# A layer of scan attention and a mixture of experts in one kernel: six wide shared slots first, six lone expert blocks in a row, weights asked for ahead of rows, and another engine for the last sums

## The chip, the cores and the metric

The kernel runs on one core of a Trainium2 chip. The metric is the time of one execution on the device in microseconds (us); the median of three runs is compared. A core has TensorE (PE, matrix products; PEld is its weight load), VectorE (DVE), ScalarE (ACT), GpSimd (POOL) and SyncE (SP), each with its own instruction stream that runs in order; they meet at semaphores. Here SP issues almost all DMAs (SPq in the rows), and POOL issues the gathers and scatters.

## The reference

```
x = x + attn(layernorm(x))      # x: 4 x 1024 x 256, 4096 rows in all
x = x + ffn(layernorm(x))

attn: h = rmsnorm(.)*gamma;  q, kv, a = split(h @ w_qkva.T);  a = sigmoid(a)
      y[t] = a[t]*y[t-1] + kv[t];  return q*y
ffn:  logits = rows @ router_w.T             # 7 routed experts, the best 2 per row
      w = softmax(the two logits)
      mixed = sum over both of w * (silu(g)*u) @ w_down[e]   # g, u = rows @ w_gate[e], w_up[e]; hidden 1024
      mixed += the same form with the shared expert, for all rows
```

## The kernel before, in words

Each float32 product is made from three products of rounded parts (high x high, high x low, low x high), so every weight needs a rounded copy (ACT, `round_w`, L809) and a remainder (`w_lo`: POOL's `split_lo`, L627, for gate and down, DVE's `split_up`, L1694, for up). Raw weights come into `w_raw`, which lies where the remainder will be.

After the attention part (to about 105 us) the expert work is one sequence of *slots* of 256 rows, numbered n. TensorE runs a slot alone (`slot`), or two of them as a *quad* of 512 rows (`quad`): eight steps j, each with 12 gate and up products (L1145, or L1101 in a slot), then the down product for the first and the second pair of row tiles. For the down product there is a wide form (`down_wide`, L1123 and L1126: one product of 512 columns, one of 256) and a narrow one (L1167: three of 256). TensorE may begin step j only when DVE has *gated* step j-2 (silu times up, L1733, after ACT's silu, L865 or L837). Then ACT rounds the gated values (L872, L844) and DVE takes the remainder (L1739).

The order of the slots, all written out by hand:

* n = 0, 1: shared expert, slots. n = 2, 4, 6, 8: shared expert, quads. Between their steps DVE works out the routing (functions in `betweens`: places, one-hot `hot_rows` and `hot_cols` for eight lists, `take_lists`, `take_targets`, `owners`), and TensorE turns each one-hot pair into a list (`list_part`, L1076).
* n = 10, 11: the first two *lone* blocks: 128 rows of one expert with weights of its own, in plain float32 (`lone`, L1187 and L1195), weights in `w_spare` (`load_lone`, L449 and L452 on SP). That memory holds the routing's tables before.
* n = 12 (`LATE`): a shared quad. n = 14 to 17: four more lone blocks.
* from `R0` = 18: 12 routed quads, then 8 routed slots (`PAIRED`), a new expert's weights for each of these 20 *turns*.
* `NB0`: two last shared quads. While they run, each row's two expert results come back from DRAM (`got`, `load_got`, L539 and L542 on SP), are weighed and added. Of 32 row tiles, DVE mixes 12 (`mix`, L1679, two instructions a tile); ACT weighs the other 20 (`weigh`, L924) and POOL adds them (L714, L716) into `resid`, which SP stores.

SP's order in the loop over the eight routed slots is: `load_down` for the next turn, `put_and_load` (store gathered rows once POOL's gather has landed, then load them turned, L457 and L463), and only then `load_gate_up` for the turn after the next (L414), which needs the end of this slot's gate and up products. Before the first lone block SP does: put and load of the first two lone blocks' rows, put of two more, wait for `routed`, `load_lone(0)` (L449), the rows of n = 12, 13, `load_lone(1)`.

POOL's order in one of those turns is `split_lo` of gate, gather, `split_lo` of down, scatter. The last stores wait until the sums for their rows are made.

Of the kernel before, what the change touches and what calls it, by code (L numbers as in the profile page):

```python
# [11 lines left out]
ALU = mybir.AluOpType  # L12
# [10 lines left out]
def preln_scan_moe_kernel(nc, x, w_qkva, gamma, router_w, w_gate, w_up, w_down,  # L23
# [9 lines left out]
    JH = H // P  # L33
# [21 lines left out]
    assert len(LONES) == NS and R0 % 2 == 0 and NS % 2 == 0 and TURNS % 2 == 0  # L55
# [7 lines left out]
    assert OTHERS[0] <= 4 and OTHERS[3] == 0  # L63
# [26 lines left out]
    with ExitStack() as ctx:  # L90
# [213 lines left out]
        others_summed = sem("others_summed")  # L304
        others_mixed = sem("others_mixed")
# [52 lines left out]
        def _(sp):  # L358
# [116 lines left out]
            for n in range(2, FIRST_LONE):  # L475
                load_x(n, n, z_dram, n % 2)
# [35 lines left out]
            for j in range(PAIRED):  # L512
                r, n, u = QUADS + j, R0 + 2 * QUADS + j, j % 2
                load_down(r + 1, 1 - u, n, shared_rows if r + 1 == TURNS else None)
                v = n + 4 - R0
# [4 lines left out]
                if r + 2 <= TURNS:  # L520
                    load_gate_up(r + 2, u, n + 1, shared_rows if r + 2 == TURNS else None)
# [27 lines left out]
            sp.wait_ge(mixed, TOP * (ST + OTHERS[0]))  # L549
# [3 lines left out]
            sp.wait_ge(mixed, TOP * (ST + OTHERS[0] + ST))  # L553
            load_got(3)
            store_own(1)
            for j in (1, 2):
                sp.wait_ge(others_mixed, FROM[j + 1] - FROM[1])
                store_others(j)
# [5 lines left out]
        def _(pool):  # L564
# [140 lines left out]

            for j in (1, 2):
                for b in range(2):
                    many = OTHERS[j] // 2
                    ps_ = slice(ST + b * many, ST + (b + 1) * many)
                    t = FROM[j] + b * many  # L710
                    done = FROM[j] - FROM[1] + (b + 1) * many
                    rows, sums = resid[:, t:t + many, :], got[:, j % 2, ps_, 0, :]
                    pool.wait_ge(weighed, TOP * done)
                    pool.tensor_tensor(sums, sums, got[:, j % 2, ps_, 1, :], ALU.add).then_inc(others_summed, many)  # L714
                    pool.wait_ge(others_summed, done)
                    pool.tensor_tensor(rows, rows, sums, ALU.add).then_inc(others_mixed, many)  # L716

        @block.scalar
        def _(act):
# [176 lines left out]
            for n in range(2, FIRST_LONE - 2, 2):  # L896
                quad(n, n % 4, early=True)
            quad(FIRST_LONE - 2, (FIRST_LONE - 2) % 4, turns=(), early=True)
            for i in range(2):
                lone(i)  # L900
            quad(LATE, LATE % 4, turns=())
# [16 lines left out]
            def weigh(j, ps_):  # L918
# [8 lines left out]
            quad(NB0, NB0 % 4, between={6: lambda: weigh(1, (ST,)), 7: lambda: weigh(1, (ST + 1,))})  # L927
            weigh(1, range(ST + 2, ST + OTHERS[1]))
            quad(NB0 + 2, (NB0 + 2) % 4, turns=(), between={
                j: lambda j=j: weigh(2, (ST + j,)) for j in range(JH)})  # L930
            weigh(2, range(ST + JH, ST + OTHERS[2]))

        @block.tensor
        def _(pe):
# [195 lines left out]
            def quad(n, h, buf, m=None, between=(), skip=NS, ahead=2, early=False):  # L1130
# [29 lines left out]
                for t in range(ST, 2 * ST):  # L1160
                    for j in range(JH):
                        if not early:
# [42 lines left out]
            for n in range(2, FIRST_LONE, 2):  # L1205
# [3 lines left out]
            for i in range(2):  # L1209
                lone(i)  # L1210
# [719 lines left out]
```

## Time and the profile before

| | us |
|---|---|
| median of three runs | 1050.58 (1049.94 to 1053.31) |
| the profiled execution, whole | 1051.96 |
| its span, first to last instruction | 1050.2 |
| PE / PEld / DVE busy | 990.5 / 859.6 / 594.0 |
| ACT / POOL busy | 474.5 / 419.2 |
| mean granted TensorE clock | 0.975 |

Busy time of TensorE is that of pipelined instructions, whose modelled ends overlap; a stage's length and the idle time before a group tell more. The granted clock is a share of 2.4 GHz, 0.5 being 1.2 GHz.

### The profile page before, as it was taken

The page shows a single profiled execution, that of the slowest core. Times are in us where ns is not written, and L with a number is a line of the kernel's source. Part 1 is how long each engine was busy: PE and PEld are TensorE (multiplying, and loading weights), DVE is VectorE, ACT ScalarE, POOL GpSimd, SP SyncE. Part 2 cuts the span into 40 slices and gives each one's busy share as a digit, 9 for nine tenths or more (in the row PEclk, how much of TensorE's full clock was granted, in tenths as well). Part 3 has the DMA queues.
Part 4 walks back from the last instruction along what each step waited for, and adds up shares of the span by engine and source line. Part 5 has one row for each costly group of instructions (what it writes and reads, how often), then busy time and mean ns, then how long its engine had stood idle before and what let it go on. Part 6 is the DMA issues. An engine that isn't in the chain of part 4 may idle for free.

```text
span 1050.2 us, 15774 instructions
## 1 busy us (share of the span) xinstructions
PE 990.5 (94%) x5517; PEld 859.6 (82%) x5517; DVE 594.0 (57%) x1048; ACT 474.5 (45%) x754; POOL 419.2 (40%) x267
## 2 busy tenths in 40 slices
PE   7999999999969999999999999999999798999966
PEld 6788988788868998888888888888889688898755
DVE  7987677778514244445644456444564343555744
ACT  4555343422213325544655446544464444765532
POOL 2335000000201233546556464654646565674304
PEclk9999999999989999999999999999999898999979
DMA  9333200000297675464345543455444556673362
GB/s 311 101 81 81 81 21 21 21 1 2 56 315 259 222 243 170 160 195 153 117 169 170 190 153 112 168 172 190 133 129 158 173 175 214 223 257 98 113 229 71
DMA packets 145905, 155.05 MB, mean 148 GB/s; under 512 B 75321, under 2 KB 134210, under 8 KB 138690
## 3 DMA queue, kind: packets, MB, share of 16 engines
q1 hardware_dynamic: 139120, 136.08, 39.8%
q0 software_dynamic: 6720, 18.36, 5.5%
q8 instruction: 27, 0.44, 0.2%
q14 instruction: 20, 0.16, 0.1%
q10 hardware_dynamic: 18, 0.01, 0.0%
HBM read 127.67 MB, written 26.74 MB: 147 GB/s over the span
## 4 chain that ended last, share of the span: by engine, by line
PE 67%; DVE 11%; issue 8%; POOL 5%; DMA 4%; ACT 2%; SPq 1%; DVEq 0%; POOLq 0%; ACTq 0%
PE ps L1145 32%; PE ps L1123 11%; PE ps L1126 6%; PE ps L1101 5%; PE ps L1187 4%; PE ps L1007 3%; POOL w_both L627 3%; PE ps L1195 2%; DMA got<-expert_rows 2%; DVE y_sb L1333 2%; PE ps L991 1%; DVE resid L1679 1%; PE ps L1167 1%; DVE h_early L1733 1%; DVE h_lo L1739 1%
## 5 line engine op out<-in xcount | busy, mean ns | idle before, releaser
L1145 PE MATMUL ps<-xs_hi,w_both 128*128 128x512 f32 x1216 | 384.7, 394 | 12.5 <-DVE ps L1733 11.8
L1145 PEld LDWEIGHTS ps<-xs_hi,w_both 128*128 128x128 f32 x1216 | 230.6, 190 | 63.2 <-DVE ps L1733 13.1
L627 POOL TENSOR_TENSOR w_both<-w_raw,w_both 128x2048 fp32r<-128x2048 f32 x45 | 224.2, 4981 | 129.7 <-ACT w_both L809 121.2
L1123 PE MATMUL ps<-w_both,h_hi 128*128 128x512 f32 x704 | 250.2, 399 | 1.0 <-DVE h_lo L1739 0.9
L1145 PE MATMUL ps<-xs_lo,w_both 128*128 128x512 f32 x608 | 238.6, 392 | 0.0
L1126 PE MATMUL ps<-w_both,h_lo 128*128 128x256 f32 x704 | 197.5, 281 | 0.0
L1739 DVE TENSOR_TENSOR h_lo<-ps,h_hi 128x512 fp32r<-128x512 f32 x152 | 105.1, 692 | 126.9 <-ACT h_hi L872 80.3
L651 POOL DMA_INDIRECT x_stage<-z_rows,idx_x x70 | 73.1, 1044 | 240.4 <-DVE idx_x L1651 156.4
L1733 DVE TENSOR_TENSOR ps<-ps,silu 128x512 f32<-128x512 f32 x152 | 106.2, 699 | 109.2 <-ACT silu L865 79.1
L1123 PEld LDWEIGHTS ps<-w_both,h_hi 128*128 128x128 f32 x704 | 132.5, 188 | 33.6 <-DVE h_lo L1739 1.8
L865 ACT ACTIVATE silu<-ps 128x512 f32<-128x512 f32 x152 | 90.7, 597 | 135.4 <-PE ps L1145 135.3
L1101 PE MATMUL ps<-xs_hi,w_both 128*128 128x256 f32 x640 | 126.3, 296 | 17.7 <-DVE ps L1733 16.8
L809 ACT ACTIVATE w_both<-w_raw 128x1024 fp32r<-128x1024 f32 x126 | 130.5, 1053 | 25.1 <-DMA w_raw<-in_L_ffn_w_gate_dram 25.0
L1145 PEld LDWEIGHTS ps<-xs_lo,w_both 128*128 128x128 f32 x608 | 115.5, 190 | 23.4
L1126 PEld LDWEIGHTS ps<-w_both,h_lo 128*128 128x128 f32 x704 | 133.0, 189 | 0.7
L1101 PEld LDWEIGHTS ps<-xs_hi,w_both 128*128 128x128 f32 x640 | 106.6, 202 | 19.8 <-DVE ps L1733 17.6
L664 POOL DMA_INDIRECT expert_rows<-y_rows,idx_y x70 | 69.6, 995 | 132.6 <-DMA expert_rows<-y_rows,idx_y 81.6
L872 ACT ACTIVATE h_hi<-ps 128x512 fp32r<-128x512 f32 x120 | 71.8, 598 | 71.4 <-DVE ps L1733 71.3
L1101 PE MATMUL ps<-xs_lo,w_both 128*128 128x256 f32 x320 | 93.9, 293 | 0.0
L1101 PEld LDWEIGHTS ps<-xs_lo,w_both 128*128 128x128 f32 x320 | 64.7, 202 | 0.0
L1809 DVE TENSOR_TENSOR y_rows<-ps,y_rows 128x512 f32<-128x512 f32 x24 | 16.6, 692 | 75.2 <-ACT y_rows L888 59.5
L1187 PE MATMUL ps<-xs_lone,w_spare 128*128 128x128 f32 x384 | 45.5, 281 | 9.1 <-issue 9.1
(225 smaller groups left out, 1055.4 us busy)
## 6 DMA issues: line engine op xcount, KB each, us to landing
w_raw<-in_L_ffn_w_gate_dram SPq DMA_DIRECT2D x20, 1024.0 KB, 5.0
w_raw<-in_L_ffn_w_up_dram SPq DMA_DIRECT2D x20, 1024.0 KB, 7.3
w_raw<-in_L_ffn_w_down_dram SPq DMA_DIRECT2D x20, 1024.0 KB, 7.0
sorted_rows<-x_stage SPq DMA_DIRECT2D x32, 256.0 KB, 2.2
x_rows<-sorted_rows SPq DMA_DIRECT2D x128, 64.0 KB, 2.0
w_spare<-in_L_ffn_w_up_dram SPq DMA_DIRECT2D x6, 1024.0 KB, 5.2
w_spare<-in_L_ffn_w_gate_dram SPq DMA_DIRECT2D x6, 1024.0 KB, 9.5
w_spare<-in_L_ffn_w_down_dram SPq DMA_DIRECT2D x6, 1024.0 KB, 11.3
```

The lines of the kernel that those rows point to most:

```text
L627: pool.tensor_tensor(w_lo[buf][:, k, :], w_raw[buf][:, k, :], w_hi[buf][:, k, :].bitcast(F32), ALU.subtract).then_inc(wlo_ready[k], 1)
L651: pool.indirect_dma_start(x_stage[:, i % 2, t, :], None, z_dram, bass.IndirectOffsetOnAxis(ap=idx_x[:, c:c + 1], axis=0), bounds_check=N - ...
L809: ins = act.activation(w_hi[buf][:, k, cols], w_raw[buf][:, k, cols], ACT.Copy)
L865: act.activation(silu[:, par, :, :], ps[:, 2 * par, :].rearrange("p (j n) -> p j n", j=2), ACT.Silu).then_inc(silu_ready, 1)
L872: act.activation(h_hi[:, j, :].rearrange("p (j n) -> p j n", j=2), h32_of(par, early), ACT.Copy).then_inc(hhi_ready, 1)
L1101: last = pe.matmul(o, w[:, part, at[kd]:at[kd] + P], unit(xx, h)[:, kd, :], start=i == 0, stop=i == len(terms) - 1)
L1123: pe.matmul(ps[:, 4 + t, :].rearrange("p (b d) -> p b d", d=D), h_hi[:, j, t * P:(t + 1) * P], both[:, :, 2, j * D:(j + 1) * D], start=j = ...
L1126: last = pe.matmul(ps[:, 4 + t, 0:D], h_lo[:, j, t * P:(t + 1) * P], hi[:, 2, j * D:(j + 1) * D], start=False, stop=j == JH - 1)
L1145: last = pe.matmul(ps[:, 2 * (j % 2) + part, :], w[:, part, kd * H + j * P:kd * H + (j + 1) * P], xx[:, h // 2, kd, :], start=i == 0, stop ...
L1187: last = pe.matmul(o, w[:, part, at:at + P], x[:, kd, 0:P], start=kd == 0, stop=kd == KD - 1)
L1733: dve.tensor_tensor(h32_of(par, early), up, silu[:, par, :, :], ALU.mult).then_inc(gated, 1)
L1739: dve.tensor_tensor(out, h32_of(par, early), hi.bitcast(F32), ALU.subtract).then_inc(h_ready, 1)
```

## The change

All twelve slots before the lone blocks are shared ones (n = 2 to 10 in quads), and the six lone blocks follow in a row. The routing steps are spread over the quads n = 2 to 8: the first one-hot pair moves from the end of n = 2 into n = 4, `take_lists` is cut in two (`sum_lists` at step 3 of n = 8, the rest at 6), `take_targets` goes to step 7 and `owners` to the end of n = 8. SP asks for the weights of the first two lone blocks together, and for the first routed turn's weights right behind the last shared quad. In the eight routed slots SP issues `load_gate_up` before `put_and_load`. The second half of the quad at n = 10 and of the last two quads has the narrow down product. POOL no longer adds expert results: ACT weighs 15 tiles, DVE sums and adds those in groups of 5 and mixes the other 17.

```diff
-    FIRST_LONE = SA - 2
-    LATE = SA
-    LONES = [n for n in range(FIRST_LONE, R0) if n not in (LATE, LATE + 1)]
+    LONES = list(range(SA, R0))
+    WEIGHED = 5
...
@@ sync
             sp.wait_ge(routed, 1)
-            load_lone(0)
-            for u in range(2):
-                load_x(LATE + u, SA - 2 + u, z_dram, u)
-            load_lone(1)
+            for i in range(2):
+                load_lone(i)
             for i in range(4, 6):
                 put_x(i)
             for i in range(2, 4):
                 load_sorted(i)
-                load_lone(i)
-            for i in range(4, 6):
-                load_sorted(i)
             for i in range(NS, NS + 2):
                 put_x(i)
-            load_gate_up(0, 0, LATE + 2)
-            load_down(0, 0, LATE + 2)
-            for i in range(4, 6):
-                load_sorted(i + 2)
-                load_lone(i)
+            load_gate_up(0, 0, SA)
+            load_down(0, 0, SA)
+            for i in range(4, NS + 2):
+                load_sorted(i)
+                load_lone(i - 2)
...
                 load_down(r + 1, 1 - u, n, shared_rows if r + 1 == TURNS else None)
+                if r + 2 <= TURNS:
+                    load_gate_up(r + 2, u, n + 1, shared_rows if r + 2 == TURNS else None)
                 v = n + 4 - R0
                 if v < ROUTED:
                     put_and_load(v, u, v // 2)
                 else:
                     load_x(n + 4, SA + v - ROUTED, z_dram, u)
-                if r + 2 <= TURNS:
-                    load_gate_up(r + 2, u, n + 1, shared_rows if r + 2 == TURNS else None)
...
@@ gpsimd
-            for j in (1, 2):
-                for b in range(2):
...
-                    pool.wait_ge(weighed, TOP * done)
-                    pool.tensor_tensor(sums, sums, got[:, j % 2, ps_, 1, :], ALU.add).then_inc(others_summed, many)
-                    pool.wait_ge(others_summed, done)
-                    pool.tensor_tensor(rows, rows, sums, ALU.add).then_inc(others_mixed, many)
...
@@ scalar
-            quad(NB0, NB0 % 4, between={6: lambda: weigh(1, (ST,)), 7: lambda: weigh(1, (ST + 1,))})
-            weigh(1, range(ST + 2, ST + OTHERS[1]))
+            quad(NB0, NB0 % 4)
+            weigh(1, range(ST, ST + OTHERS[1]))
             quad(NB0 + 2, (NB0 + 2) % 4, turns=(), between={
-                j: lambda j=j: weigh(2, (ST + j,)) for j in range(JH)})
-            weigh(2, range(ST + JH, ST + OTHERS[2]))
+                j: lambda j=j: weigh(2, (ST + OTHERS[2] - WEIGHED + j - 2,)) for j in range(2, 2 + WEIGHED)})
...
@@ tensor
-            for i in range(2):
-                lone(i)
-            quad(LATE, LATE % 4, 0, skip=2, ahead=0)
-            for i in range(2, NS):
+            for i in range(NS):
                 lone(i)
...
-            quad(NB0, NB0 % 4, 0, m=TURNS + 1)
-            quad(NB0 + 2, (NB0 + 2) % 4, 0, ahead=0)
+            quad(NB0, NB0 % 4, 0, m=TURNS + 1, wide=False)
+            quad(NB0 + 2, (NB0 + 2) % 4, 0, ahead=0, wide=False)
...
@@ vector
+            def sum_weighed(j, p0, nth):
+                rows, a, b = rows_of_weighed(j, p0)
+                dve.wait_ge(weighed, TOP * WEIGHED * nth)
+                dve.tensor_tensor(a, a, b, ALU.add).then_inc(summed, 1)
+            def add_weighed(j, p0, nth):
+                rows, a, b = rows_of_weighed(j, p0)
+                dve.wait_ge(summed, nth)
+                mixes[0] += WEIGHED
+                dve.tensor_tensor(rows, rows, a, ALU.add).then_inc(mixed, WEIGHED)
...
+            last = ST + OTHERS[2] - WEIGHED
             quad(NB0 + 2, (NB0 + 2) % 4, shared=SA + 2, between={
-                4: lambda: mix(2, (0,)), 5: lambda: mix(2, (1,)), 6: lambda: mix(3, (0,)), 7: lambda: mix(3, (1,))})
+                0: lambda: sum_weighed(1, ST, 1), 1: lambda: add_weighed(1, ST, 1),
+                2: lambda: sum_weighed(1, ST + WEIGHED, 2), 3: lambda: add_weighed(1, ST + WEIGHED, 2),
+                4: lambda: mix(2, (0,)), 5: lambda: mix(2, (1,)), 6: lambda: mix(2, (2,)), 7: lambda: mix(2, (3,)),
+                "down": lambda: mix(2, range(4, last)),
+                "half": lambda: (sum_weighed(2, last, 3), add_weighed(2, last, 3), mix(3, (0, 1)))})
```

## Rows read from the trace of the kernel before

**Rows 1.** Who PE and ACT waited for: total us, times, longest.

```profile
PE ps L1101 <- DVE ps L1733: 16.8, 4, 7.8
PE ps L1145 <- DVE ps L1733: 11.8, 3, 6.7
PE ps L1187 <- issue: 9.1, 1, 9.1
...
ACT w_both L809 <- DMA w_raw<-in_L_ffn_w_gate_dram: 25.0, 4, 9.9
```

**Rows 2.** Busy time by stretch, cut at stage borders.

```profile
core 0: us, PE busy (x) PEld busy (x) DVE busy (x) ACT busy (x) POOL busy (x), PEclk, DMA share, GB/s
148.84:182.06 33.22, 33.22 (x178) 28.67 (x177) 26.22 (x64) 11.76 (x19) 0.00 (x0) 1.00 0.07 17
...
217.94:252.66 34.72, 34.72 (x211) 29.61 (x209) 24.68 (x49) 10.60 (x18) 0.00 (x0) 1.00 0.00 1
...
288.61:297.90 9.29, 0.17 (x3) 0.03 (x1) 0.69 (x1) 0.00 (x0) 1.01 (x1) 0.63 0.94 288
...
353.86:396.07 42.21, 42.21 (x322) 40.58 (x321) 14.51 (x30) 13.93 (x27) 12.12 (x5) 1.00 0.69 225
396.07:793.60 397.53, 397.53 (x1923) 334.00 (x1921) 206.96 (x311) 205.07 (x312) 216.47 (x119) 1.00 0.49 161
...
811.07:905.27 94.20, 77.43 (x513) 73.48 (x513) 38.77 (x56) 44.99 (x64) 56.01 (x24) 0.87 0.59 198
905.27:956.79 51.52, 51.52 (x387) 49.29 (x386) 29.44 (x42) 33.60 (x48) 36.34 (x13) 1.00 0.54 184
...
990.92:1041.81 50.89, 39.08 (x162) 30.99 (x160) 30.24 (x36) 17.20 (x37) 18.92 (x7) 0.87 0.36 119
1041.81:1050.20 8.39, 0.00 (x0) 0.00 (x0) 1.38 (x2) 0.00 (x0) 1.27 (x1) 0.71 0.66 219
```

**Rows 3.** The timeline of SP's DMA issues: start, us, what.

```profile
287.04 0.36 SPq L449 DMA_DIRECT2D w_spare<-in_L_ffn_w_up_dram  x1
```

**Rows 4.** The same view in the stage of routed slots.

```profile
814.61 0.40 SPq L457 DMA_DIRECT2D sorted_rows<-x_stage  x1
...
819.45 0.37 SPq L414 DMA_DIRECT2D w_raw<-in_L_ffn_w_gate_dram  x1
```

**Rows 5.** DMA issues by tensor: count, size, median us to landing.

```profile
w_raw<-in_L_ffn_w_gate_dram SPq DMA_DIRECT2D x20, 1024.0 KB, 5.0
...
w_spare<-in_L_ffn_w_gate_dram SPq DMA_DIRECT2D x6, 1024.0 KB, 9.5
```

**Rows 6.** One line of code each: duration ns min/median/max, first and last start.

```profile
L1679 DVE SCALAR_TENSOR_TENSOR resid<-got,mix_w,resid x24: 473/484/3201, 978.7 to 1035.7; 128x256 f32<-128x256 f32 x24
```

**Rows 7.** The same view, of the remainder of the up weights.

```profile
L1694 DVE TENSOR_TENSOR w_both<-w_raw,w_both x42: 1209/1217/1781, 370.8 to 955.2; 128x1024 fp32r<-128x1024 f32 x42
```

**Rows 8.** Groups of POOL's instructions from 984 to 1050 us.

```profile
L714 POOL TENSOR_TENSOR got<-got 128x1280 f32<-128x1280 f32 x4 | 12.2, 3043 | 55.4 <-ACT got L924 55.4
```

**Rows 9.** DVE's timeline in the last two quads.

```profile
960.51 0.70 DVE L1733 TENSOR_TENSOR ps<-ps,silu 128x512 f32<-128x512 f32 x1 [2.13 <-ACT silu L865]
961.88 0.69 DVE L1739 TENSOR_TENSOR h_lo<-ps,h_hi 128x512 fp32r<-128x512 f32 x1 [0.67 <-ACT h_hi L872]
963.12 0.70 DVE L1733 TENSOR_TENSOR ps<-ps,silu 128x512 f32<-128x512 f32 x1 [0.55 <-ACT silu L865]
...
984.43 12.28 DVE L1679 SCALAR_TENSOR_TENSOR resid<-got,mix_w,resid 128x256 f32<-128x256 f32 x10
...
1032.28 0.99 DVE L1679 SCALAR_TENSOR_TENSOR resid<-got,mix_w,resid 128x256 f32<-128x256 f32 x2
```

**Rows 10.** SP's timeline at the return of expert results and at the end.

```profile
997.16 0.51 SPq L539 DMA_DIRECT2D got<-expert_rows  x1
...
1043.11 0.37 SPq L525 DMA_DIRECT2D out_dram<-resid  x1
```

**Rows 11.** ACT's timeline, the first weighing of the second return.

```profile
1009.90 0.91 ACT L924 ACTIVATE got<-got,mix_w 128x256 f32<-128x256 f32 x2 [6.08 <-DMA got<-expert_rows]
```

More of the change, by code:

```diff
@@ L474, in _ @@
             sp.wait_ge(z_out[NC - 1], 16)
-            for n in range(2, FIRST_LONE):
+            for n in range(2, SA):
                 load_x(n, n, z_dram, n % 2)
@@ L1128, in down_wide, with quad @@
                 return last
-            def quad(n, h, buf, m=None, between=(), skip=NS, ahead=2, early=False):
+            def quad(n, h, buf, m=None, between=(), skip=NS, ahead=2, wide=True):
                 pe.wait_ge(x_split, n - skip + 2)
@@ L1636, in hot_cols, with sum_lists @@
                 dve.sem_inc(hot_made, 1)
-            def take_lists():
+            def sum_lists():
                 dve.wait_ge(hot_used, CHUNKS)
@@ L1801, in quad @@
                     between["half"]()
-                if shared is not None and early:
+                if shared is not None:
                     add_narrow(n + 1, shared * ST + ST)
-                elif shared is not None:
-                    add_wide(n + 1, shared * ST + ST, 6)
                 if routed is not None:
@@ L1871, in _ @@
                 2: {0: pair_targets, 3: lone_places, 6: lone_targets, 7: find_pairs, "down": move_all,
-                    "half": first_lists},
-                4: {0: lambda: hot_rows(1), 3: lambda: hot_cols(1), 7: lambda: pick(1),
-                    "down": lambda: (halves_of(1), lists(2)), "half": lambda: lists(3)},
+                    "half": lambda: first_places(0)},
+                4: {0: lambda: hot_rows(0), 3: lambda: hot_cols(0), 6: lambda: hot_rows(1), 7: lambda: hot_cols(1),
+                    "down": lambda: (first_places(1), lists(2)), "half": lambda: lists(3)},
                 6: {0: lambda: hot_rows(4), 3: lambda: hot_cols(4), 6: lambda: hot_rows(5), 7: lambda: hot_cols(5),
-                    "down": lambda: (lists(6), owners()), "half": lambda: lists(7)}}
-            for n in range(2, FIRST_LONE - 2, 2):
-                quad(n, n % 4, turns=ahead_of(n), shared=n, early=True, skip=0, between=betweens[n])
-            n = FIRST_LONE - 2
-            quad(n, n % 4, shared=n, early=True, skip=0, between={
-                3: take_lists, 6: take_targets, "down": lambda: turn(n, n % 4, 2, loads(n + 2), 0, "lone"),
-                "half": lambda: turn(n, n % 4, 3, loads(n + 3), 0, "lone")})
-            for i in range(2):
+                    "down": lambda: lists(6), "half": lambda: lists(7)},
+                8: {3: sum_lists, 6: take_lists, 7: take_targets, "down": owners}, 10: {}}
+            for n in range(2, SA, 2):
+                quad(n, n % 4, turns=ahead_of(n), kind="pair" if n + 2 < SA else "lone", shared=n,
+                     early=n + 2 < SA, skip=0, between=betweens[n])
+            for i in range(3):
                 lone(i)
-            quad(LATE, LATE % 4, turns=ahead_of(LATE), kind="lone", shared=SA - 2, skip=2)
-            lone(2)
             lone(3, between={2: lambda: split_half(1, 0, 0), 3: lambda: split_half(1, 0, 1)})
```

50 lines of the change are left out of this document (24 added, 26 removed).

## Prediction

> **What bounds the kernel.** I read the waits of TensorE first, then cut its timeline at the stage borders and asked for each stretch, then read SP, ACT, DVE and POOL around each hole. TensorE sets the pace nearly everywhere: from 396.07 to 793.60 it is busy without a gap and twelve routed quads take 397.53 us, 33.13 each [rows 2]. Three holes are left.
>
> First, 288.61 to 297.90: TensorE stands before the first lone block [rows 1, 2]. SP asked for that block's weights only at 287.04 [rows 3], because they stand in its order behind eight list and row steps, and the lists are ready late in the quad n = 8.
>
> Second, the routed slots. The last three take 51.52 us, 17.17 each; the four before them, from 811.07 to 905.27, take 94.20, 25.5 more than four times that [rows 2]; TensorE's longest wait there is 7.8 us. ACT waited four times, 25.0 us in all, for raw gate weights [rows 1]. TensorE's 16.8 us for DVE's gate is the same wait one engine on: ACT is stuck in `round_w`, so silu, so the gate, are late. Why the weights are late is in SP's rows: it stored gathered rows at 814.61 and asked for weights only at 819.45 [rows 4], though the gate and up products that free the place ended 11.5 us into the slot, near 805. The three good slots are those whose weights were asked for behind `load_x`, which waits for no gather.
>
> Third, the last quad: 50.89 us from 990.92 for work that elsewhere takes 33.13 [rows 2]. DVE spent 12.28 us on ten mixes from 984.43 [rows 9], and TensorE waited 11.8 us for gates, with a mean clock of 0.87 [rows 1, 2].
>
> **Stage A, 148.84 to the first routed quad at 396.07: 247.23 us.** TensorE's work stays the same: five quads, eight lists, six lone blocks. A quad with the narrow second half and no list took 33.22. The quad n = 6 had four lists, spaced as the new n = 4 and n = 6 have them, and took 34.72, so a list with its small stalls is (34.72 - 33.22)/4 = 0.375. Four lone blocks in a row took 42.21, 10.55 each [all rows 2]. The sum is 5 x 33.22 + 8 x 0.375 + 6 x 10.55 = 232.4, a gain of 14.8. It has 9.3 of the hole, some 1.6 of half clock behind it, and the stalls that DVE's routing steps made in n = 4 and n = 8.
>
> The cover has to hold. By its steps `take_lists` ends some 23 us into n = 8, as before (about 273), and SP should reach `load_lone` 2 us later than before, near 289; the lone blocks begin at about 318. So two loads of 9.5 us [rows 5] lie behind n = 10, with 29 us of room. `owners` (some 4 us) moves to where TensorE has 11 us of down products to do. In the row of lone blocks, gate and up for block i+2 are asked for when those of block i end, 7.1 us into it, so 2 x 10.55 - 7.1 = 14.0 us before need; at 9.5 us to landing 4.5 are left. The first routed turn's weights go into the 11 us of n = 10's down products and at the first block's start, before that queue. The bound above is the rival of starving below; a gain beyond 14.8 has no source.
>
> **Stage B, the eight routed slots, 793.60 to 956.79: 163.19 us.** With `load_gate_up` first, every slot can ask at its 11.5th microsecond. Gate weights need 5.0 to land [rows 5]; ACT wants them 3.5 us into the next slot, 17.17 - 11.5 + 3.5 = 9.2 after the issue, so 4 are over. What is moved behind, four stores and 32 row loads in all (half of them by `load_x`), is for the slot four on and has a whole slot of slack. But SP now blocks on the gather when it should issue the next `load_down`: in the first slot the store came 21 us after its start at 793.60 [rows 4], and with the row loads SP is free 4 us later, 8 after the point where down weights may be asked for. With some 5 to land they are there 13 us into the slot, when ACT, done with its four steps, comes to round them; a few us more only push POOL's split of them, which TensorE wants 11.5 us into the next slot. In later slots the gather should come some 4 us sooner. POOL was busy 56.01 us in four of these slots, 14.0 of 17.17 [rows 2], so it keeps up. I take no stall: 8 x 17.17 + 0.3 = 137.7, a gain of 25.5. From below, a gain is bounded by that; from above, the rival on SP's order.
>
> **Stage C, from 956.79 to the end at 1050.20: 93.41 us.** POOL's sums go, eight instructions of about 3.0 us [rows 8]. A mix takes 0.484 in the median but up to 3.201 [rows 6], and that one spans a POOL sum; two took 0.99 together at 1032.28 [rows 9], while ACT weighed and POOL did not add. So the ten mixes should take 5 us instead of 12.28, all of the first quad's 16 fit behind its down products (about 8 of 11 us), and it takes 33.2. The page SBUF — State Buffer of the Trainium skill (section Who interferes with whom) says that a VectorE instruction with two inputs in SBUF and a GpSimd instruction that reads SBUF exclude each other for whole instructions. The 3.201 agrees; by that rule the new sums, two inputs each, would be slowed too, if POOL had any work then, and it has none.
>
> In the last quad DVE gets four new steps at j = 0 to 3, of 1280 elements. None is in the trace. 1024 took 1.217 [rows 7], so in proportion 1.52; a mix of 256 at 0.484 [rows 6] gives 2.42 as the upper bound, and 1.22 is the lower. I take 1.5, nearest in size. A gate and its remainder hold DVE for 2.06 (960.51 to 962.57) and come every 2.73 [rows 9, 2]. With a sum the period is 3.56, with two mixes 3.03. The gates of steps 0 to 4 put that of step 5 late by 4 x 0.83 + 0.30 = 3.6; about 1.0 of that is TensorE's two-step lead, so it stalls 2.5 in all, in pieces under 1 us. The quad's TensorE work ends at 33.2 + 2.5 = 35.7 after its start. DVE: the first gate starts at 3.7, the eighth at 3.7 + 4 x 3.56 + 3 x 3.03 = 27.0; its remainder and two mixes end at 30.0, six mixes at 33.0, the add of the first half at 34.4, sum and add of the last five tiles at 37.5. Only then is the last big store free. Before, it was issued at 1043.11 [rows 10] and the end came 7.1 later; the same 1.75 MB follow now, so 44.7. The one-instruction add of the second half falls under it. The stage: 33.2 + 44.7 = 77.9, a gain of 15.5.
>
> The second return of rows (`got`) must be there: 12.7 us from 997.16 to ACT's start at 1009.90 [rows 10, 11]. It now starts when twelve mixes are done, some 30 us into the first quad, and lands at 43; ACT wants it at about 45.5. The narrow halves cost TensorE 0.1 us each and are in these sums.
>
> **Sum.** 14.8 + 25.5 + 15.5 = 55.8. The profiled execution's whole time was 1051.96, 1.76 beyond its span, so 996.2; the median of the runs is 1.4 below it: 994.8.
>
> **Rivals.**
>
> *SP's new order bites (0.13).* A gather that lands later than I think holds back `load_down`, ACT waits for down weights at the end of its steps and everything behind shifts. It decides when down weights land more than some 7 us after ACT wants them. For it: four stores of rows and their waits stand there now, and scatters and weights share the DMA engines. Against: it has a slot's length. With half of the excess in the first four slots left (25.5/2), the time is 1007; with a fifth, 1000.
>
> *The row of lone blocks starves (0.09).* Four instead of two sets of 3 MB must come at 10.55 us each. Against: the last four ran like that with DMA at 0.69 of its time [rows 2]; for it: at 9.5 us a load there is less than 5 to spare. At 3 us late for two blocks, with as much again for half clock behind a wait, about 6: 1001.
>
> *The clock falls in the last quad (0.12).* The new stalls are short but come step after step. A spell at 1.2 GHz of some 7 us costs 3.5 in products; about that much reaches the end: 998. In the last quad before, the clock was 0.87 in the mean, but behind waits of 6.7 us; from 905 to 956 it was 1.00 without any [rows 1, 2]. The Trainium skill (TensorE: Matmul & The Clock Gate, section A second HAM failure mode: psum-queue depth-cycling) tells of a kernel whose small idles between groups made the clock swing; no row here has such idles to test it, which is why it has this chance.
>
> *The new sums are dearer, or got comes late (0.05).* At 2.42 a sum, six of them, four ahead of the gates: some 5.5 more, 1000.
>
> *Slower (0.02).* Six lone blocks of small products in a row at 1.2 GHz would take 63.3 us more and the change would lose 7.5: 994.8 + 63.3 = 1058. It decides from 5.3 blocks on. Four in a row had a clock of 1.00 [rows 2], so it is nearly excluded.
>
> **Numbers.** My forecast has 0.59, its own range 991 to 999. The range that reaches over clock, dear sums and the lesser form of the first two rivals is 989 to 1004. One can tell 0.3%, about 3 us, from no change. Only the last rival is slower: 0.02; nothing ends near zero except several together: 0.01; faster 0.97.
>
> **What would show it.** Stage A: no hole before L1187, the first lone block near 318 at full clock, six of 10.6 each; wrong if PE waits for a DMA there. Stage B: no wait of ACT for gate weights, slots of 17.2; wrong if one for down weights is in its place. Stage C: mixes all near 0.48, sums near 1.5, gaps under 1 us in the last quad's first eight steps, the last big store some 37.5 us into it.

## The result, and the profile after

The changed kernel takes 1000.01 us in the median of four runs (998.73 to 1001.46), beside 1050.26 for the kernel before on the same chip: a ratio of 0.9517, with a 95% interval of 0.9491 to 0.9544. The forecast was 994.8. The profiled execution took 998.79, its span 997.0, where the prediction's sum gave 996.2.

Busy time by stretch says where that went. The first six rows are stage A (four shared quads with the routing, the quad n = 10, the row of lone blocks), then the twelve routed quads, the eight routed slots (stage B), the two last quads and the end (stage C). They answer to [rows 2]; columns as there.

```profile
150.03:183.22 33.19, 33.19 (x178) 28.68 (x177) 26.20 (x64) 11.76 (x19) 0.00 (x0) 1.00 0.07 16
183.22:217.71 34.49, 34.39 (x203) 29.34 (x201) 26.24 (x47) 10.48 (x18) 0.00 (x0) 1.00 0.07 16
217.71:252.42 34.71, 34.71 (x214) 29.59 (x210) 27.67 (x40) 10.59 (x18) 0.00 (x0) 1.00 0.07 16
252.42:286.12 33.70, 33.70 (x189) 28.93 (x187) 23.42 (x60) 10.59 (x18) 3.32 (x3) 1.00 0.07 19
286.12:319.31 33.19, 33.19 (x179) 28.68 (x178) 14.03 (x23) 9.58 (x16) 5.05 (x5) 1.00 0.74 239
319.31:385.85 66.54, 64.21 (x482) 60.63 (x481) 17.60 (x41) 17.66 (x37) 20.29 (x13) 1.00 0.90 295
385.85:783.60 397.75, 397.74 (x1922) 333.84 (x1921) 206.75 (x311) 204.91 (x312) 216.37 (x118) 1.00 0.49 161
783.60:920.95 137.35, 137.35 (x1026) 131.44 (x1025) 78.51 (x112) 90.02 (x128) 100.53 (x41) 1.00 0.66 221
920.95:954.17 33.22, 33.22 (x178) 28.67 (x177) 22.23 (x41) 19.15 (x39) 6.05 (x3) 1.00 0.57 181
954.17:989.31 35.14, 34.43 (x178) 28.33 (x176) 26.46 (x39) 12.98 (x26) 0.00 (x0) 1.00 0.44 144
989.31:997.00 7.69, 0.00 (x0) 0.00 (x0) 2.85 (x6) 0.00 (x0) 0.00 (x0) 0.78 0.72 239
```

| stage | before | forecast | after |
|---|---|---|---|
| start of stage A | 148.84 | 148.84 | 150.03 |
| A, to the first routed quad | 247.23 | 232.4 | 235.82 |
| twelve routed quads | 397.53 | 397.53 | 397.75 |
| B, eight routed slots | 163.19 | 137.7 | 137.35 |
| C, to the end | 93.41 | 77.9 | 76.05 |

B and C are as forecast, C 1.9 better. Stage A is 3.4 too long, and all but 0.2 of it lies in one row: the six lone blocks took 66.54 where 63.3 stood in the sum. The later start of stage A is not the change's: it varied from 148.6 to 150.0 over all the kernels below that share the part before it.

In the waits of TensorE the hole before the lone blocks, the waits for gates in slots and the 11.8 us in the last quad [rows 1] are gone. What is left of them in the changed kernel, with a new wait that is spread over three lone blocks ("issue" means that this view names nothing that the engine waited for):

```profile
PE ps L1168 <- issue: 2.3, 3, 1.7
PE ps L1126 <- DVE ps L1714: 0.7, 2, 0.3
```

The landings of the weights say what it was: the third block's gate weights, asked for at 332.26, landed 10.0 us later, at 342.26, and its first product began at 342.36.

**The lone blocks.** SP's DMA issues around them (start, us, what) show the order that did it:

```profile
293.75 0.36 SPq L449 DMA_DIRECT2D w_spare<-in_L_ffn_w_up_dram  x1
...
300.90 8.07 SPq L425 DMA_DIRECT2D sorted_rows<-x_stage  x2
309.07 4.71 SPq L437 DMA_DIRECT2D x_rows<-sorted_rows  x8
320.88 3.58 SPq L427 DMA_DIRECT2D sorted_rows<-x_stage  x2
325.21 0.38 SPq L414 DMA_DIRECT2D w_raw<-in_L_ffn_w_gate_dram  x1
...
331.80 0.37 SPq L449 DMA_DIRECT2D w_spare<-in_L_ffn_w_up_dram  x1
```

and POOL's gathers at the same time, the last bracket being the idle time before each:

```profile
294.93 1.01 POOL L646 DMA_INDIRECT x_stage<-z_rows,idx_x  x1 [0.30 <-issue]
316.75 1.01 POOL L646 DMA_INDIRECT x_stage<-z_rows,idx_x  x1 [20.81 <-DMA sorted_rows<-x_stage]
```

Read them upward. The third block's weights should have been asked for when the first block's gate and up products end, at 319.31 + 7.1 = 326.4; they were asked for at 331.80. Ahead of them SP had the rows of the fifth block, 3.47 us of issuing from 327.58 on, and the first routed turn's weights, at 325.21, though their place was free at about 308, 21.8 us into n = 10. And ahead of those it stood before the last two stores of gathered rows, until 320.88, because POOL's gather for them began only at 316.75: it had waited 20.81 us for an earlier store of rows, which SP had issued at 300.90, behind the 6 MB of the first two lone blocks. Issuing that one store took SP 6.70 us. So the first turn's 3 MB fell into the row of lone blocks. The DMA share in the three blocks from 329.91 was above 1:

```profile
319.31:329.91 10.60, 10.60 (x83) 10.19 (x81) 2.80 (x7) 1.53 (x4) 2.03 (x2) 1.00 0.61 200
329.91:342.36 12.45, 10.77 (x82) 10.03 (x80) 2.11 (x6) 2.30 (x6) 1.51 (x2) 1.00 1.04 378
342.36:353.48 11.12, 10.84 (x81) 10.11 (x81) 2.11 (x6) 5.45 (x9) 4.64 (x5) 1.00 1.06 364
353.48:364.68 11.20, 10.84 (x80) 10.10 (x81) 4.41 (x8) 3.89 (x8) 5.58 (x2) 1.00 1.09 335
```

The Trainium skill (DMA: Bandwidth & Descriptors, section Queues, rings and completion order) says that each DMA engine consumes the descriptors of one issuing engine's ring in order. The landings here agree with it: the last of the six weight transfers ahead of the store landed at 315.77, and the gather that waited for the store began 0.98 us later. In two kernels below, `turn0_first` and `old_routing`, the two times are 315.29 and 316.34, and 308.48 and 309.60. The first 5 of the 20.81 us lie before the store was issued at all. Which bytes each DMA engine moved when, no view here shows.

**The routed slots.** Here are SP's issues of one slot, with the gate weights asked for at 795.53, 11.9 us into it, and the store of rows behind them:

```profile
795.53 0.34 SPq L414 DMA_DIRECT2D w_raw<-in_L_ffn_w_gate_dram  x1
...
804.95 0.40 SPq L457 DMA_DIRECT2D sorted_rows<-x_stage  x1
807.14 1.90 SPq L463 DMA_DIRECT2D x_rows<-sorted_rows  x4
809.80 0.41 SPq L420 DMA_DIRECT2D w_raw<-in_L_ffn_w_down_dram  x1
```

ACT's 25.0 us of waiting for gate weights [rows 1] are 1.8 over the whole kernel, and those lie in the first routed quad, at 391.34, whose weights were the ones asked for at 325.21; in the slots it waits twice for down weights, 0.46 and 0.33 us. The store came 21.3 us after the start of the first slot, as before (21), and hurt nothing.

**The last two quads.** DVE's timeline, which answers to [rows 9], has the ten mixes in 4.17 instead of 12.28 us, and the new sums at 1.48:

```profile
945.74 4.17 DVE L1660 SCALAR_TENSOR_TENSOR resid<-got,mix_w,resid 128x256 f32<-128x256 f32 x10
...
959.78 1.48 DVE L1885 TENSOR_TENSOR got<-got 128x1280 f32<-128x1280 f32 x1
961.17 0.69 DVE L1714 TENSOR_TENSOR ps<-ps,silu 128x512 f32<-128x512 f32 x1
...
988.39 1.49 DVE L1892 TENSOR_TENSOR resid<-resid,got 128x1280 f32<-128x1280 f32 x1
```

From the sum's start the gate follows in 1.39 us, without idle time: in these steps DVE sets the pace, with 0.66 us of waiting for ACT's rounding in each. The last big store became free at 989.9, 35.7 into the quad, and the end came 7.1 later.

### The profile page after: what moved, and what is told of

It reads as the page before. It is cut to its first block, busy times and chain, and to the rows that moved or that the text cites. A ratio compares the mean times of both kernels' runs of the same rounds, so it can differ in the third digit from the quotient of the medians.

```text
span 997.0 us, 15861 instructions
## 1 busy us (share of the span) xinstructions
PE 976.9 (98%) x5565; PEld 849.9 (85%) x5565; DVE 591.1 (59%) x1061; ACT 470.1 (47%) x744; POOL 393.9 (40%) x259
## 4 chain that ended last, share of the span: by engine, by line
PE 88%; DVE 7%; issue 2%; ACT 1%; DMA 1%; SPq 0%; DVEq 0%
PE ps L1126 39%; PE ps L1104 15%; PE ps L1082 11%; PE ps L1107 7%; PE ps L1168 4%; PE ps L988 4%; PE ps L1148 3%; PE ps L1176 2%; DVE y_sb L1311 2%; PE ps L972 1%; DVE hT_lo L1271 1%; DVE h_lo L1720 1%; PE ps L999 1%; ACT h_hi L855 1%; DMA resid<-in_L_attn_x_dram 1%
## 5 line engine op out<-in xcount | busy, mean ns | idle before, releaser
L1126 PEld LDWEIGHTS ps<-xs_hi,w_both 128*128 128x128 f32 x1216 | 228.2, 188 | 50.6 <-DVE ps L1714 2.7
L1104 PE MATMUL ps<-w_both,h_hi 128*128 128x512 f32 x656 | 233.0, 398 | 0.1
L1107 PE MATMUL ps<-w_both,h_lo 128*128 128x256 f32 x656 | 184.1, 281 | 0.0
L1104 PEld LDWEIGHTS ps<-w_both,h_hi 128*128 128x128 f32 x656 | 123.3, 188 | 30.2 <-DVE h_lo L1720 0.4
L1126 PEld LDWEIGHTS ps<-xs_lo,w_both 128*128 128x128 f32 x608 | 114.2, 188 | 23.0
L1107 PEld LDWEIGHTS ps<-w_both,h_lo 128*128 128x128 f32 x656 | 123.9, 189 | 0.7
L1082 PE MATMUL ps<-xs_hi,w_both 128*128 128x256 f32 x640 | 117.9, 284 | 0.8 <-DVE xs_lo L1343 0.8
L1082 PEld LDWEIGHTS ps<-xs_hi,w_both 128*128 128x128 f32 x640 | 99.9, 189 | 1.6 <-issue 1.2
L1082 PE MATMUL ps<-xs_lo,w_both 128*128 128x256 f32 x320 | 90.6, 283 | 0.0
L1082 PEld LDWEIGHTS ps<-xs_lo,w_both 128*128 128x128 f32 x320 | 60.5, 189 | 0.0
L1675 DVE TENSOR_TENSOR w_both<-w_raw,w_both 128x1024 fp32r<-128x1024 f32 x42 | 49.5, 1218 | 0.0
## 6 DMA issues: line engine op xcount, KB each, us to landing
w_spare<-in_L_ffn_w_down_dram SPq DMA_DIRECT2D x6, 1024.0 KB, 14.2
```

The lines of the kernel that those rows point to most:

```text
L1082: last = pe.matmul(o, w[:, part, at[kd]:at[kd] + P], unit(xx, h)[:, kd, :], start=i == 0, stop=i == len(terms) - 1)
L1104: pe.matmul(ps[:, 4 + t, :].rearrange("p (b d) -> p b d", d=D), h_hi[:, j, t * P:(t + 1) * P], both[:, :, 2, j * D:(j + 1) * D], start=j = ...
L1107: last = pe.matmul(ps[:, 4 + t, 0:D], h_lo[:, j, t * P:(t + 1) * P], hi[:, 2, j * D:(j + 1) * D], start=False, stop=j == JH - 1)
L1126: last = pe.matmul(ps[:, 2 * (j % 2) + part, :], w[:, part, kd * H + j * P:kd * H + (j + 1) * P], xx[:, h // 2, kd, :], start=i == 0, stop ...
```

## The experiments

All ratios are to the kernel before, measured beside it on the same chip (medians 1050.58 to 1051.23). The runs were made on three chips, and the changed kernel was not measured again beside them, so a difference of one or two us between two medians below says little. The lengths of stages in the profiled executions say more: the quad n = 6 took 34.7 us in all thirteen profiles.

**The middle part alone.** The kernel before, with gate and up asked for ahead of the rows in the routed slots.

```diff
                 load_down(r + 1, ...)
+                if r + 2 <= TURNS:
+                    load_gate_up(r + 2, ...)
...
                     put_and_load(v, u, v // 2)
-                if r + 2 <= TURNS:
-                    load_gate_up(r + 2, ...)
```

> The kernel before, with one edit: in the eight routed slots SP issues load_gate_up ahead of put_and_load. If the gate weights were late only because they stood behind the gathered rows in SP's order, the stage goes from 163.2 to about 137.4 us and the whole becomes 25.5 us faster, near 1025. Rival (POOL's splits or the late down load take over as the bound): the stage keeps 10 us or more of its excess, the whole is 1035 or more, and ACT waits for down weights.

Measured: 1025.77, ratio 0.9763 (0.9747 to 0.9779), 24.8 faster. The eight slots took 137.70 together (busy time by stretch, columns as in [rows 2]):

```profile
793.60:931.30 137.70, 137.64 (x1027) 131.41 (x1026) 78.50 (x112) 90.04 (x128) 102.34 (x41) 1.00 0.66 221
```

and the list of waits has no gate weights for ACT in it. The order of two requests in SP's stream was the whole of the 25.5 us, and the rival on SP's new order has no case: the later `load_down` fits.

**The ending alone.** The kernel before, with the new split of the expert sums and the narrow halves of the last two quads.

> The kernel before with the new ending alone: POOL adds nothing, ACT weighs 15 tiles, DVE sums them and mixes 17, the last two quads have the narrow second half. If the parts are independent the gain is that of the last stage in the changed kernel, 93.4 - 76.1 = 17 us, near 1033. Rival (the gain needed the earlier stages): under 12.

Measured: 1035.12, ratio 0.9845 (0.9821 to 0.9868), 15.5 faster in the medians, near the 17 expected and above the rival's 12. The stage itself shows the 17: the two last quads and the end take 33.22, 35.13 and 7.72 together, 76.07 for 93.41. The profiled execution lost 1.65 of it again in the quad n = 4, which the edit does not touch, at a mean clock of 0.95 (36.16 us at 1.00 in the kernel before). Here are that quad, the last quad and the end:

```profile
182.40:220.21 37.81, 36.02 (x203) 30.45 (x201) 28.84 (x50) 10.55 (x18) 0.00 (x0) 0.95 0.06 15
991.79:1026.92 35.13, 34.43 (x178) 28.32 (x176) 26.46 (x39) 12.98 (x26) 0.00 (x0) 1.00 0.43 144
1026.92:1034.64 7.72, 0.00 (x0) 0.00 (x0) 2.84 (x6) 0.00 (x0) 0.00 (x0) 0.75 0.71 238
```

That the medians give just the 15.5 of the prediction is chance.

**Without POOL's sums.** The kernel before, in which POOL's eight sums are left out and ACT and DVE do what they did.

```diff
@@ gpsimd
-                    pool.wait_ge(weighed, TOP * done)
-                    pool.tensor_tensor(sums, sums, got[...], ALU.add)...
-                    pool.tensor_tensor(rows, rows, sums, ALU.add)...
@@ sync
-                sp.wait_ge(others_mixed, FROM[j + 1] - FROM[1])
+                sp.wait_ge(weighed, TOP * (FROM[j + 1] - FROM[1]))
```

> The kernel before without POOL's eight sums at the end; the expert results of 20 row tiles are weighed but not added, so this part of the computation is left out. DVE's 24 mixes are the same. If POOL's sums are what slows the mixes, all 24 take near 0.48 us, the ten from the end of the first of the last two quads take 5 us instead of 12.3, and the last stage shrinks by 15 us or more. Rival (ACT's weighing or the DMA traffic slows the mixes): their mean stays near 1.0 us and the last stage gains less than 5.

Measured: 1036.41, ratio 0.9857 (0.984 to 0.9873), 14.2 faster; the last stage took 78.9 us for 93.4, a little less than the 15 us or more that were expected. No mix is long any more; the line of the mixes, between 474 and 486 ns where [rows 6] had up to 3201:

```profile
L1666 DVE SCALAR_TENSOR_TENSOR resid<-got,mix_w,resid x24: 474/480/486, 979.9 to 1025.2; 128x256 f32<-128x256 f32 x24
```

So the mixes were long because POOL added. But a second wait of the old ending comes to light: its last quad still took 39.95 us, not 33.1, since ACT's first weighing of the second return stands ahead of the second silu and waits 5.37 us for `got`:

```profile
1003.18 0.91 ACT L911 ACTIVATE got<-got,mix_w 128x256 f32<-128x256 f32 x2 [5.37 <-DMA got<-expert_rows]
1003.99 0.57 ACT L852 ACTIVATE silu<-ps 128x512 f32<-128x512 f32 x1
```

```profile
992.87:1032.82 39.95, 35.79 (x162) 29.29 (x160) 17.91 (x30) 17.11 (x36) 0.00 (x0) 0.91 0.54 179
```

TensorE waits 4.2 us at a stretch for that gate, and the quad (the second fence, busy time by stretch) has a mean clock of 0.91. The new ending cures it too, by having ACT weigh from step 2 on. The prediction had put the last quad's waits down to the ten mixes alone.

**Middle and ending together, without the new start.**

> The changed kernel with its old order of shared quads and lone blocks and the old routing steps (both other parts are in). What it lacks against the changed kernel is what order and routing bring: 247.2 us before and 235.8 after in that stage, so 11 us slower than the changed kernel, near 1010. Rival (parts overlap, stages are not additive): under 7 or over 15.

Measured: 1009.43, ratio 0.9607 (0.9591 to 0.9623); the changed kernel is 9.4 faster. Stage A's share of the gain is therefore 9.4 in the medians and 11.4 between the profiled executions (247.2 for 235.8), where the prediction had 14.8. The three parts add up: in the medians 24.8 + 15.5 + 9.4 = 49.7, where before and after differ by 50.25; in the stages 25.5 + 17.3 + 11.4 = 54.2, where the spans differ by 53.2 and the start of stage A was 1.2 later.

**POOL busy beside the mixes.** The changed kernel, with four additions of 128x1024 on POOL, in its own memory, from the first mix on.

> The changed kernel with four instructions added on POOL that read and write an unused tile in SBUF (128 x 1024, some 2.4 us each) from the first mix on; nothing waits for them but the next of them. If a POOL instruction holds off VectorE's mixes, the ten mixes that took 4.2 us take about 12, the first of the last two quads passes its lateness on, and the whole is 3 to 9 us slower. Rival (it was the waits for POOL's result that cost before, not its being busy): mixes stay at 0.48 and the time is the same.

Measured: 999.11, ratio 0.9505 (0.948 to 0.953): no dearer than the changed kernel within the spread of the medians. Counted from the start of n = 2 to the end, the profiled execution took 1.4 us more, 848.4 for 847.0. The contention itself is plain in the timelines of POOL and of DVE:

```profile
942.14 7.92 POOL L704 TENSOR_TENSOR x_stage<-x_stage 128x1024 f32<-128x1024 f32 x4 [15.96 <-DVE resid L1665]
...
941.59 2.73 DVE L1665 SCALAR_TENSOR_TENSOR resid<-got,mix_w,resid 128x256 f32<-128x256 f32 x2
...
946.20 7.32 DVE L1665 SCALAR_TENSOR_TENSOR resid<-got,mix_w,resid 128x256 f32<-128x256 f32 x10
```

POOL's four additions took 1.92 us each, not the 2.4 expected. Two mixes take 2.73 for 1.00, ten take 7.32 for 4.17, the longest 2.2 us, so the rival (mixes stay at 0.48) is out. The last quad grew from 35.14 to 36.76, and the rest of the 4.9 us that the mixes lost fell on time that DVE had to spare: in the changed kernel it stood idle for 1.24 and 2.74 us between the last mixes and the last quad's first gate. So the expected 3 to 9 us did not come: slower mixes cost only what goes beyond DVE's slack. Before, the ten mixes took 12.28 us ahead of a gate, beside POOL's longer sums (3.04 us each), which is more than this slack; that reading was not tested by itself.

**First turn's weights first.** The changed kernel with one call moved.

```diff
+            load_gate_up(0, 0, SA)
             for i in range(NS, NS + 2):
                 put_x(i)
-            load_gate_up(0, 0, SA)
```

> The changed kernel, with the gate and up load of the first routed turn issued ahead of the store of the seventh and eighth gathered rows. In the changed kernel SP reached that load only at 325.2, behind the stores, though its place was free at 308; its 3 MB then shared the DMA engines with the weights of the third and fourth lone block, and TensorE lost 3.2 us over the six blocks. If that is the cause, the blocks run at 10.6 us each and the whole is 3 us faster, near 997. Rival (3 MB per 10.6 us is too much for the row of blocks whatever stands before): same within 1 us.

Measured: 994.60 (994.08 to 996.15), ratio 0.9464 (0.9443 to 0.9486): 5.4 faster than the changed kernel in the medians. The gate weights are asked for at 313.51 and the third block's at 328.56, and the row of lone blocks, as one stretch, has no wait:

```profile
318.77:382.20 63.43, 63.43 (x483) 60.98 (x481) 18.02 (x41) 17.76 (x37) 20.30 (x13) 1.00 0.87 290
```

63.43 for 66.54 is 3.1, the 3 expected. Of it 2.3 were waits, and the rest lies in the products around them, where the last product of a block no longer overlaps the first of the next. The changed kernel has two runs near 998.8, the profiled one among them, and two near 1001.3; what the latter two lost no profile shows, and with it the rest of the 5.4.

**The old places of the routing.** The changed kernel, with DVE's routing steps and TensorE's lists where they stood before.

```diff
@@ sync
+            sp.wait_ge(listed, 2)
@@ tensor
-                at = {4: {6: [0], JH: [1]}, ..., 8: {0: [6], 1: [7]}}
+                at = {4: {1: [0], JH: [1]}, ..., 8: {0: [6], 2: [7]}}
@@ vector
... (n = 2 to 6, likewise)
-                8: {3: sum_lists, 6: take_lists, 7: take_targets, "down": owners}
+                8: {3: lambda: (sum_lists(), take_lists()), 6: take_targets}
```

> The changed kernel with the routing steps where they were: first pair of one-hots at the end of n = 2, first list at step 1 of n = 4, owners in n = 6, take_lists whole at step 3 of n = 8, take_targets at 6. If the spreading brings what the quads n = 4 and n = 8 show (35.9 and 36.0 us before, 34.5 and 33.7 after), it is 3 to 3.7 us slower than the changed kernel. Rival (spreading is hidden or the stalls came from the lone blocks' neighbourhood): within 1 us.

Measured: 997.97 (997.59 to 998.18), ratio 0.9495 (0.947 to 0.9519): in the medians 2.0 faster, not some 3 slower, though the interval overlaps that of the changed kernel. Two effects that work against each other show in the busy time of three stretches, n = 4, n = 8 and the lone blocks:

```profile
181.79:217.95 36.16, 34.40 (x202) 29.31 (x201) 28.78 (x50) 10.55 (x18) 0.00 (x0) 1.00 0.07 16
252.65:288.35 35.70, 34.16 (x190) 28.87 (x187) 23.35 (x48) 10.43 (x18) 5.71 (x5) 1.00 0.15 38
...
321.60:385.00 63.40, 63.40 (x482) 60.95 (x481) 18.02 (x41) 17.78 (x37) 18.28 (x11) 1.00 0.85 292
```

The quads lose 1.67 and 2.00, as expected, and the lone blocks win 3.14. Together stage A is 0.5 us longer, 236.4 for 235.8, not shorter. The profiled execution was 1.2 us faster all the same, because its stage A began at 148.63 and not at 150.03, in a part that both kernels share. So no gain of the old places is shown; what is shown is that they cost 0.5 us instead of 3.7.

The list of rows that the gathers need is written by a cast on DVE. It starts 17.9 us after the start of n = 8 with the old places and 24.1 with the new ones (DVE's timeline, first of the changed kernel, then of this one):

```profile
276.51 0.20 DVE L1632 CAST idx_x<-rows_f 128x70 int32<-128x70 f32 x1
```

```profile
270.51 0.20 DVE L1633 CAST idx_x<-rows_f 128x70 int32<-128x70 f32 x1
```

The extra wait of SP in the diff belongs to the old places: `owners` comes early there, and the weights may not land on the routing's tables before the second list is written. Everything that SP does before the lone blocks moved with the cast: their weights were asked for at 287.62 instead of 293.75, the first turn's at 318.23, before the row, instead of 325.21, within it.

**Both at once.** The kernel turn0_first with the old places of the routing.

> The changed kernel with the first routed turn's gate and up weights asked for ahead of the last two puts (the kernel turn0_first) and, besides, the routing's steps where the kernel before had them. It asks what the spreading is worth once the row of lone blocks no longer starves. Theory A (the spreading is worth what the stalls in n = 4, 6 and 8 cost, and the row of lone blocks cannot give any of it back now): the three quads take 36.2 + 34.7 + 35.7 = 106.6 as in the kernel old_routing, against 102.9 in the changed kernel, the lone blocks 10.6 each in both: 3.7 slower than turn0_first, 998.3. Theory B (what counts is how early the lists are there; they come at the same place in the stream of rows but TensorE comes later, so the old places never cost anything): equal to turn0_first, 994.6.

Measured: 998.17 (997.95 to 999.38), ratio 0.9497 (0.9484 to 0.951). With the run before, it makes a table of four (us), the median first, then stage A in the profiled execution:

| | rows first, then the first turn | the first turn first |
|---|---|---|
| routing spread | 1000.01; 235.8 | 994.60; 232.7 |
| routing in its old places | 997.97; 236.4 | 998.17; 238.0 |

Each cure alone makes the row of lone blocks 63.4 to 63.5 long. Once the first turn's weights are out of the way, spreading is worth 3.6 us in the medians and 5.3 in stage A, of which 1.6 are a slower clock in one quad: 3.7 at equal clock, as theory A had it. While they aren't, it is worth 0.5 in stage A. In the profile of this last kernel n = 4 took 37.80 at a mean clock of 0.95, where the same code had taken 36.16 at 1.00 in the run before:

```profile
181.94:219.74 37.80, 36.02 (x203) 30.47 (x201) 28.83 (x50) 10.53 (x18) 0.00 (x0) 0.95 0.06 15
```

**Small sums.** The changed kernel with the four sums in the last quad's first four steps cut to 8 columns.

> The changed kernel with DVE's four sums at steps 0 to 3 of the last quad cut down to 8 of their 1280 columns each, with all their waits and signals as they were; rows of ten tiles lack their expert results. It asks what the four sums cost by their length. Theory A (DVE is late for TensorE through them): TensorE's waits in the last quad go, its gate and up part falls from 23.6 to about 21.8, and the end comes some 1.8 us earlier: 998.2. Rival B (DVE's own chain up to the last big store sets the end, and the four sums lie on it in full): 4 x 1.42 = 5.7 earlier, 994.3. Rival C (neither: the last own rows and their stores set it behind TensorE, whose waits are only the spacing of gates): no change, 1000.

Measured: 995.63 (995.11 to 996.97), ratio 0.9473 (0.946 to 0.9486). The medians differ by 4.4, between the two theories, but the changed kernel's runs lie 2.7 apart. The busy time of the last quad and of what follows it says more:

```profile
954.37:987.71 33.34, 33.33 (x178) 28.62 (x176) 22.36 (x40) 13.21 (x26) 0.00 (x0) 1.00 0.47 151
987.71:994.60 6.89, 0.00 (x0) 0.00 (x0) 2.00 (x5) 0.00 (x0) 0.00 (x0) 0.67 0.80 266
```

The quad is 1.80 shorter, which is theory A, and the tail 0.80 besides, which theory A did not have: 2.6 in all. The other 1.8 of the medians no stretch shows. DVE's own 5.7 us do not lie on the end in full: with short sums it waits up to 0.6 us for ACT's silu in each of these steps, at TensorE's pace.

**Two better endings.** On turn0_first, the last big store is cut in two, with two tiles' own rows stored between the pieces.

```diff
-            for j in (1, 2):
-                sp.wait_ge(mixed, MIXED[j + 1])
-                store_others(j)
-            for j in (2, 3):
-                store_own(j)
+            sp.wait_ge(mixed, MIXED[2])
+            store_others(1)
+            cut = FROM[3] - WEIGHED
+            for t0, t1, have in ((FROM[2], cut, MIXED[3] - WEIGHED), (cut, FROM[3], MIXED[3])):
+                sp.wait_ge(mixed, have)
+                sp.dma_start(out_t[:, t0:t1, :], resid[:, t0:t1, :]).then_inc(outs, 16)
+                if t0 != cut:
+                    store_own(2)
+            store_own(3)
```

> The kernel with the early gate and up load, and the last big store cut in two: five of its ten row tiles go out as soon as DVE has mixed them, with the first half's own rows behind them, the other five after their sum. The last store's own transfer then starts some 4 us sooner and the end after it moves 1 to 2 us: 2 us less than with the early load alone, near 995. Rival (the end hangs on DVE's last instructions and a fixed time of a store, not on bytes): within 0.5 us of the early load alone.

Measured: 992.90 (991.93 to 993.16), ratio 0.9446 (0.9425 to 0.9467), 1.7 faster than the early load alone; the last quad is as long (35.13), and from its end to the last instruction it takes 5.51 us for 7.71. Then the first sum moves out of step 0 into DVE's gap behind the quad before.

> The kernel better (first turn's weights first, last big store cut in two) with the first of DVE's new sums moved out of step 0 of the last quad, into the gap that DVE has behind the quad before it. The sums stand at steps 1 and 3, the add at 0. Theory A (the three short waits of TensorE in the last quad, 0.7 us and what lies around them, some 1.8 us against a quad without sums, come from four sums in a row ahead of the gates): with three in that place about 0.9 of it goes, 992.0. Rival (the end is set by DVE's own work after the gates and by the stores, not by TensorE): no change, 992.9.

Measured: 991.52 (991.46 to 991.78), ratio 0.9434 (0.9421 to 0.9447), 1.4 less than the kernel `better`, between medians taken on two chips. In the profiled executions the last quad took 34.36, 0.77 less than there (0.9 expected), and the end behind it did not change (busy time by stretch):

```profile
949.90:984.26 34.36, 34.09 (x178) 28.39 (x176) 26.65 (x39) 12.99 (x26) 0.00 (x0) 1.00 0.53 174
```

This is the fastest kernel of the study, 59.7 us under the kernel before and 8.5 under the changed one.

## Why the prediction was right, and where it missed

The sum was off by 2.6 us in the profiled execution: 1.2 of the start, 3.4 of stage A and 0.2 of the routed quads too little, 0.4 and 1.9 of stages B and C too much. The median is 5.2 above the forecast, inside the range. Of the other 2.6 us, 1.4 are the step from the profiled execution to the median, which was taken over from the kernel before, and 1.2 its going the other way here: two of the four runs took 2.5 us more than the profiled one, and where is open.

- **The hole before the lone blocks, and the quads.** Right. The five quads took 169.28, forecast 169.1, so the quads at 33.22 hold, and a list at 0.375 us holds in the mean (0.65 each in n = 4, 0.38 in n = 6, 0.26 in n = 8). No hole stands before the first lone block, which began at 319.31, forecast 318.
- **"By its steps `take_lists` ends some 23 us into n = 8, as before."** The first half held (24.1), the second did not: in the kernel before the row list was written 18.1 us into the quad, and 17.9 with the old places. The prediction missed that the change delays it by some 6 us, and with it SP's `load_lone`, at 293.75 and not 289.
- **"The first routed turn's weights go into the 11 us of n = 10's down products and at the first block's start, before that queue."** This is the step that failed. They were asked for at 325.21, 17 us after their place was free, behind two stores of gathered rows. The row of lone blocks starved and took 3.2 us more than its 63.3; the rival with a chance of 0.09 came half true, at half its price: the lateness came, and the half clock behind it did not (1.00 in all six blocks). Two different edits show that it was the late asking: moving one call ends the wait, and so does bringing the list forward by 6.2 us, which moves more than this one request.
- **Stage B.** Right in mechanism and size, 137.35 for 137.7, and on its own 24.8 of 25.5. ACT waited for down weights twice, 0.8 us in all, and TensorE did not wait.
- **Stage C.** Right in mechanism, and 1.9 too long: 76.05 for 77.9, a gain of 17.4 for 15.5. The mis-sized term is DVE's chain to the last big store, which came free 35.7 us into the quad and not 37.5: the sums cost 1.48 (taken: 1.5), but the period with one was 3.36, not 3.56, and the stall 1.8 us, not 2.5. The wait of ACT for `got` in the last quad before, worth some 4 us of TensorE's time, was not in the working, as its cure was contained in a quad reckoned at its plain length. The second return landed before ACT wanted it, and the clock stayed at 1.00 in the last quad (the 7 us of that rival's slow spell stand in no row), with gates 3.36 us apart in four steps where TensorE alone has 2.73.
- **Slower.** Six lone blocks of 10.6 us each at a clock of 1.00: the case has no ground.

## What to carry to other kernels

When a computation that others wait for is moved to smooth one engine, list everything that starts when it ends, down to the last DMA request in the queue: here 6.2 us of delay in a list gave back 3.1 of the 3.7 us that the smoothing had won. In a queue that runs in order, put a request whose place is already free ahead of one that must wait for another engine; here that was worth 25 us in one place and 3 to 5 in the other. And when two cures are tried, try them together too, and compare the stages and not only the medians: alone, the old places had a median 2.0 us lower and a stage A 0.5 us longer; together with the other cure they were 3.6 us worse.

## What the hardware did that was not expected

POOL's four additions of 128x1024 slowed mixes by up to 4.6 times (2.2 us for one of 0.48), as expected, and yet cost the last quad only 1.6 us. TensorE kept a granted clock of 1.00 in all last quads of the new ending, though it stalled there by 0.3 us at a time; in the old ending it had 0.87 with a longest wait of 6.7 us, and 0.91 with one of 4.2 us where POOL's sums were left out. But the quad n = 4 with the old routing places, the same code in seven profiled kernels, took 36.1 to 36.2 us at 1.00 in five of them and 37.8 at 0.95 in two, with one wait of TensorE of 1.7 or 1.8 us in each. Such a wait cost 1.6 us more in two executions of seven, and nothing here shows what decides it.

And a DMA request can hold the engine that issues it: SP spent 6.70 us on issuing one store of 128 KB behind the weights of two lone blocks (6.25 and 7.00 in `turn0_first` and `old_routing`), where the median for stores of this line is 0.43 us.
